# Masking the second attention's queries on ScalarE, padding two weights of layer 3 to 128 rows, and a new table of stages: a four-layer kernel on one core

## The reference, cut to what matters

```python
# layer 0: convolutions over tokens, cross-attention over channels (2 heads)
# layer 1: attention, 32 query heads of 8 numbers over 8 key heads, then norm; gamma, beta
# layer 2: attention of 16 heads of 16 numbers over 128 keys (context and own tokens), then the MLP
q = heads(x @ q_w + q_b);  k, v = split(concat(ctx, x) @ kv_w + kv_b)
s = q @ k.T / 16 ** 0.5 + mask              # per batch 16 heads x 64 queries x 128 keys
x = x + (softmax(s) @ v) @ out_w + out_b
x = x + gelu(rms(x) @ mlp_w1 + b1) @ mlp_w2 + b2
# layer 3: a recurrent block
xa = ln(x);  sx = shifted(xa) - xa
f = tanh((xa + sx * maa_x) @ maa_w1)        # 5 parts of 32 columns
xm_j = xa + sx * (maa_j + f_j @ maa_w2[j])  # the five mixings, a contraction over 32 each
w = exp(-exp(time_decay + tanh(xm_w @ td_w1) @ td_w2))      # decay, a contraction over 64
k, v, r = xm_k @ Wk.T, xm_v @ Wv.T, xm_r @ Wr.T;  g = silu(xm_g @ Wg.T)
for t in tokens:  a = outer(k_t, v_t);  out_t = r_t @ (u * a + s);  s = a + w_t * s
x1 = x + (groupnorm(out) * g) @ Wo.T
x = x1 + sigmoid(xr2 @ Wfr.T) * (relu(xk2 @ Wfk.T) ** 2 @ Wfv.T)   # xk2, xr2: shifted ln(x1)
```

## Time and profile before

| | |
|---|---|
| median of 3 runs | 1982.87 us (1982.61 to 1985.68) |
| the profiled execution | 1985.88 us |
| its span in the trace | 1984.2 us |
| mean granted clock of TensorE | 0.927 |
| busy, share of the span | PE 84%, PEld 52%, DVE 64%, ACT 47%, POOL 41% |
| chain that ended last | PE 58%, ACT 14%, DVE 11%, issue 8%, POOL 5%, DMA 2% |

### The profile page before, as it was taken

How to read it: one execution, slowest core, us unless ns; L and a number is a source line. 1 busy time by engine, 2 the same in 40 slices (tenths; PEclk the granted TensorE clock), 3 DMA queues, 4 the chain that set the end, 5 groups by cost and what they waited for, 6 DMA issues and landing times.

```text
span 1984.2 us, 36756 instructions
## 1 busy us (share of the span) xinstructions
PE 1676.4 (84%) x13615; PEld 1032.9 (52%) x13615; DVE 1276.6 (64%) x2183; ACT 932.2 (47%) x1831; POOL 805.1 (41%) x893
## 2 busy tenths in 40 slices
PE   5888898898988898888987989888988989888835
PEld 3565555564564555655555645646456554556203
DVE  3753469745796468845697457955689456883383
ACT  4444554544545544555445456454445454453202
POOL 4531247503573136701485034731367014750070
PEclk8998999999999999898999989998998989999757
DMA  6001014200332005210142103320052101410070
GB/s 177 2 1 34 1 23 50 38 24 1 42 37 38 18 1 64 26 27 18 22 47 29 37 1 37 41 39 18 1 60 29 27 18 19 48 23 12 0 86 11
DMA packets 73584, 60.92 MB, mean 31 GB/s; under 512 B 38960, under 2 KB 56512, under 8 KB 73408
## 3 DMA queue, kind: packets, MB, share of 16 engines
q1 hardware_dynamic: 55648, 47.99, 17.8%
q10 hardware_dynamic: 17216, 10.55, 2.1%
q0 software_dynamic: 544, 0.03, 0.0%
HBM read 20.28 MB, written 4.19 MB: 12 GB/s over the span
## 4 chain that ended last, share of the span: by engine, by line
PE 58%; ACT 14%; DVE 11%; issue 8%; POOL 5%; DMA 2%; ACTq 0%; DVEq 0%; POOLq 0%; SPq 0%
PE bank L622 24%; PE bank L761 7%; PE bank L1002 6%; PE bank L940 3%; PE bank L638 3%; PE bank L894 3%; ACT soft_ring L1141 3%; DVE late L1303 2%; DMA late<-late 2%; PE bank L701 2%; POOL soft_ring L1674 2%; PE bank L965 2%; DVE soft_ring L1450 2%; ACT soft_ring L1160 2%; ACT late L1032 2%
## 5 line engine op out<-in xcount | busy, mean ns | idle before, releaser
L1674 POOL TENSOR_TENSOR soft_ring<-soft_ring,seg_max 128x512 f32<-128x512 f32 x256 | 276.7, 1096 | 282.8 <-DVE seg_max L1456 282.1
L1160 ACT ACTIVATE soft_ring<-soft_ring 128x512 f32<-128x512 f32 x256 | 160.6, 627 | 234.9 <-POOL soft_ring L1674 223.0
L1632 POOL TENSOR_TENSOR late<-late 128x520 f32<-128x520 f32 x128 | 189.2, 1478 | 147.8 <-DMA late<-late 116.9
L1303 DVE TENSOR_TENSOR_SCAN late<-late 128x520 f32<-128x520 f32 x128 | 219.4, 1714 | 22.3 <-DVE xr L1481 6.7
L940 PE MATMUL bank<-ident,soft_ring 128*128 128x128 f32 x1024 | 170.3, 295 | 53.0 <-ACT soft_ring L1160 46.8
L940 PEld LDWEIGHTS bank<-ident,soft_ring 128*128 128x128 f32 x1024 | 116.3, 147 | 138.1 <-ACT soft_ring L1160 83.0
L1450 DVE SCALAR_TENSOR_TENSOR soft_ring<-bank,mask 128x512 f32<-128x512 f32 x256 | 164.0, 681 | 33.6 <-PE bank L761 25.9
L1456 DVE TENSOR_REDUCE seg_max<-soft_ring 128x8 f32<-128x512 f32 (+1 forms) x256 | 166.2, 674 | 5.8 <-DVE early L1514 2.1
L761 PE MATMUL bank<-early 64*128 64x512 f32 (+1 forms) x512 | 122.7, 566 | 55.4 <-ACTq L1144 51.2
L1682 POOL TENSOR_SCALAR soft_ring<-soft_ring,rden 128x256 f32<-128x256 f32 x64 | 62.2, 971 | 234.2 <-DVE rden L1423 234.2
L1032 ACT ACTIVATE late<-bank 128x512 f32<-128x512 f32 (+2 forms) x104 | 62.0, 597 | 202.1 <-PE bank L622 198.0
(11 more groups left out here) (250 smaller groups left out, 3402.5 us busy)
## 6 DMA issues: line engine op xcount, KB each, us to landing
late<-late SPq DMA_DIRECT2D x128, 260.0 KB, 4.4
c<-in_ctx ACTq DMA_DIRECT2D x8, 512.0 KB, 4.1
x<-in_x ACTq DMA_DIRECT2D x8, 512.0 KB, 5.2
out_x<-late SPq DMA_DIRECT2D x8, 512.0 KB, 2.9
mask<-in_mask_Bx1xSxS_ff ACTq DMA_DIRECT2D x16, 128.0 KB, 4.5
mask<-in_mask_BxS_ik SPq DMA_DIRECT2D x8, 256.0 KB, 3.4
w<-in_L_xattn_mlp_w SPq DMA_DIRECT2D x2, 1024.0 KB, 9.5
wkv<-in_L_xattn_kv_w SPq DMA_DIRECT2D x1, 512.0 KB, 4.4
```

Of the source, the lines that this page charges most:

```text
L1160: af(soft[:, u % SOFT, :], soft[:, u % SOFT, :], ACT.Exp).then_inc(sig("exp"), 1)
L1303: nc.vector.tensor_tensor_scan(sj[:, n % 2, :], wP[:, k, :, :].rearrange("p b t -> p (b t)"), aj[:, n % 2, :], 0.0, ALU.mult, ALU.add).the ...
L1632: tt(aj[:, n % 2, :], kP[:, k, :, :].rearrange("p b t -> p (b t)"), vj[:, n % 3, :], ALU.mult).then_inc(sig("kv_done"), 1)
L1674: tt(s, s, seg_max[:, u % SOFT, 0:segs].unsqueeze(2).broadcast_to([128, segs, 512 // segs]), ALU.subtract).then_inc(sig("sub"), 1)
```

## The change: masked queries from ScalarE, padded weights, new places

- **Queries.** `one_query` and `qring` are gone. ScalarE's drain of the queries writes them masked, twice (j = 0 and 1), into `qm`: heads of one parity each. Two heads share 32 partitions, so the scores now contract over 32 rows, and a bank of scores holds two head tiles times two batches in place of one batch with four. The mask is read for two batches at a time, and `pT2` is written accordingly. ScalarE takes 8 instructions a group in place of 4. The first half of the queries has a buffer of its own (`qm_first`).
- **Padding.** `maa2` and `td2` are filled up with zeros to 128 rows, and the products of the mixings and of the decay run over 128 rows. GpSimd zeroes 32 unused partitions of `xf` once per group (a wait for the previous group's last store ahead of it), and TensorE waits for that at a mixing.
- **Tables.** What table ScalarE has loaded is remembered from group to group.
- **Places.** Nearly every number of `PLACES` and `SCAN_PLACES` is another.

```diff
-        qring = sb("qring", [128, 2, KT, HPT // 2, L])
+        qm_first = sb("qm_first", [128, KT, NB // 2, 2, L])
...
-        q2T = cut(early, 7168, KT, NB, L)
+        qm = (qm_first, cut(early, 7168, KT, NB // 2, 2, L))
...
+                nc.gpsimd.memset(maa2[:, :, :], 0.0)
+                nc.gpsimd.memset(td2[:, :], 0.0)
...
-            "moments 2": (127, 128, 126, 121),
-            "turn 2": (132, 131, 130, 121),
-            "ffn k": (134, 133, 130, 122),
+            "moments 2": (127, 126, 125, 125),
+            "turn 2": (130, 129, 125, 128),
+            "ffn k": (133, 133, 129, 132),
...
+        loaded = [LOG_EXP]
...
                     def mix(f):
-                        rows = slice(32 * (f % 4), 32 * (f % 4) + 32)
                         for m in range(KT):
-                            product((stage, m), 512, [(maa2[rows, f // 4, 128 * m:128 * m + 128], xf[rows, f // 4, :])], "late")
+                            product((stage, m), 512, [(maa2[:, f, 128 * m:128 * m + 128], xf[:, f // 4, :])], "late")
...
-                            product((stage, m), 512, [(td2[64:64 + DD, 128 * m:128 * m + 128], xf[64:64 + DD, 1, :])], "late")
+                            product((stage, m), 512, [(td2[:, 128 * m:128 * m + 128], xf[:, 1, :])], "late")
...
-                    b = (u - UNITS) // 2
-                    pe.wait_ge(sig("k2_ready"), past("k2_ready") + 2 * (b // 4) + 2)
-                    pe.wait_ge(sig("qring_ready"), past("qring_ready") + b + 1)
+                    p, r = (u - UNITS) // 4, (u - UNITS) % 4
+                    pe.wait_ge(sig("k2_ready"), past("k2_ready") + 2 * (p // 2) + 2)
+                    pe.wait_ge(sig("q2_ready"), past("q2_ready") + p // 2 + 1)
                     side_by_side([("s", u), ("s", u + 1)], 4, lambda n, half: (
-                        qring[HALVES[half], b % 2, n // 2, 2 * (n % 2):2 * (n % 2) + 2, :], k2T[HALVES[half], n // 2, b, :]))
+                        qm[p // 2][32 * (r + half):32 * (r + half) + 32, n // 2, 2 * p % 4 + n % 2, :, :],
+                        k2T[32 * (r + half):32 * (r + half) + 32, n // 2, 2 * p + n % 2, :]))
...
                             for k in range(KT):
-                                ins = af(q2T[:, k, 4 * h:4 * h + 4, :], batches(t[:, 256 * k:256 * k + 256]), ACT.Identity, bias=v("q_b", k))
+                                for j in range(2):
+                                    ins = af(qm[h][:, k, :, j, :], batches(t[:, 256 * k:256 * k + 256]), ACT.Identity,
+                                             bias=q_bias[:, k, j:j + 1], scale=hmask2[:, j:j + 1])
...
-                def one_query(b):
-
-                    dve.wait_ge(sig("q2_ready"), past("q2_ready") + b // 4 + 1)
-                    if b >= 2:
-                        filled(("s", UNITS + 2 * b - 3))
-                    tt(qring[:, b % 2, :, :, :], q2T[:, :, b, :].unsqueeze(2).broadcast_to([128, KT, HPT // 2, L]),
-                       hmask4[:, :].unsqueeze(1).unsqueeze(3).broadcast_to([128, KT, HPT // 2, L]), ALU.mult).then_inc(sig("qring_ready"), 1)
...
+                        if before:
+                            pool.wait_ge(sig("stored"), past("stored"))
+                        link(nc.gpsimd.memset(xf[32:64, 1, :], 0.0))
+                        pool.sem_inc(sig("xf_zero"), 1)
```

More of the change, by code:

```diff
@@ L412, in _ @@
                 nc.vector.tensor_tensor(kvmask[:, :], block8[:, 0:8, 0], block8[:, 8:16, 0], ALU.add)
[L413 removed]
+                link(nc.vector.tensor_reduce(hmask2[:, :], hmask[:, :].rearrange("p (a j) -> p j a", j=2), X, ALU.add))
                 nc.vector.tensor_copy(ones2[:, 16:32], half[:, :, :].rearrange("p a b -> p (a b)"))
@@ L445, in build @@
             "moments": (0, 0, 0, 0),
[L446 to L466, removed]
-            "moments 2": (127, 128, 126, 121),
-            "normalize 2": (129, 131, 129, 121),
-            "turn 2": (132, 131, 130, 121),
-            "shift 2": (132, 131, 130, 121),
-            "ffn k": (134, 133, 130, 122),
-            "ffn r": (134, 133, 134, 128),
-            "ffn v": (134, 137, 134, 131),
+            "normalize": (3, 10, 1, 1),
+            "turn": (11, 11, 5, 1),
+            "shift": (14, 16, 12, 2),
+            "maa": (16, 16, 12, 7),
+            "mix 0": (17, 28, 18, 13),
+            "mix 1": (22, 28, 24, 13),
+            "td": (28, 30, 30, 19),
+            "k": (35, 30, 31, 19),
+            "mix 2": (35, 33, 35, 19),
+            "decay": (37, 36, 36, 19),
+            "v": (42, 40, 39, 23),
+            "mix 3": (42, 40, 42, 35),
+            "mix 4": (43, 40, 43, 36),
+            "r": (47, 44, 48, 39),
+            "g": (49, 48, 49, 41),
+            "r u k": (50, 49, 50, 41),
+            "bonus": (53, 51, 56, 57),
+            "center": (125, 122, 121, 119),
+            "variance": (125, 122, 121, 119),
+            "gate": (127, 122, 123, 119),
+            "project": (127, 126, 124, 121),
+            "moments 2": (127, 126, 125, 125),
+            "normalize 2": (127, 126, 125, 128),
+            "turn 2": (130, 129, 125, 128),
+            "shift 2": (132, 133, 128, 132),
+            "ffn k": (133, 133, 129, 132),
+            "ffn r": (133, 133, 132, 132),
+            "ffn v": (134, 133, 134, 132),
         }
         SCAN_PLACES = (
[4 rows of a table removed]
[4 rows of a table added]
         )
@@ L1519, in between @@
                             moments([xr[:, p, :] for p in (2 * h, 2 * h + 1)], stats[:, r, :], mv[:, r, :], "stats1_ready")
-                    if i == A2 - 1:
-                        for b in range(2):
-                            one_query(b)
                 def prepare(i):
@@ L1553, in prepare @@
                         dve.sem_inc(free, 1)
+                        for k in range(KT):
+                            ins = ts(q_bias[:, k, :], hmask2[:, :], v("q_b", k), None, ALU.mult)
+                        link(ins)
                         dve.sem_inc(sig("vec_ready"), 1)
@@ L1601, in vector_program @@
                     between(i)
-                    if A2 <= i < A2 + UNITS - 4 and (i - A2) % 2 == 1:
-                        one_query((i - A2) // 2 + 2)
                 if before is None:
```

34 lines of the change are left out of this document (22 added, 12 removed), and 8 rows, old and new, of the table SCAN_PLACES.

## The result

The changed kernel takes 1959.03 us (median of 4 runs, 1958.57 to 1961.88), the kernel before, measured again beside it, 1984.28. The ratio is 0.9863, 95% interval 0.9847 to 0.9879: 1.4% faster, 27 us. Forecast were 9. The direction and the range were right, the size was a third of what came.

The account below looks back on a forecast made before the run. TensorE was taken as the bound, other edits paying only through its waits; gains 3.8 less losses 3.0 gave 0.8 us a steady group, 5.6 in seven, plus group 0's 2.5: 8.1 off, forecast 1974 us, range 1950 to 1994.

Parts of the forecast that it names:

- the places' gain at the start of attention 2: TensorE's 4.67 us wait shrinks as scans and products run earlier: 0.9 us a group, bounds 0 and 4.67.
- the last block: Layer 3 of the last group alone: nothing competes there, so its time stays; no gain.
- Queries: Masking leaves VectorE: 0.65 us a group off the scores' wait in attention 2, plus 2.5 once in group 0.
- Scores over 32 rows: Attention scores: two tiles of 32 rows run side by side like those of 64, so nothing changes.
- rival 3: Score tiles of 32 rows don't run side by side: 0.6 us for each of 64 pairs, about 2012; chance 0.05.
- Padding: Mixings and decay over 128 rows: 10 fewer tile-mode changes at 0.17 us, 1.45 us a group taken; duration unchanged.
- The 0.8 for P0: GpSimd's product P0, placed ten subtractions later, no longer waits for its DMA: 0.8 us a group gained.
- P13 behind B: Recurrence behind attention 2: GpSimd's product P13 after bias row B delays scan 13; 1.6 us a group lost.
- MLP: TensorE waits 0.9 us before turn 2 and 0.9 before Wfk, less 0.4 gained: 1.4 us a group lost.
- Sum of the places: All new places: gains of 1.7 against losses of 3.0 us a group, so 9 us slower.
- Rival 1: VectorE bounds attention 2: its freed 8.3 us a group give 1917, or 1950 if half comes; chance 0.13.
- Rival 2: The new order waits at B ahead of P13 and the MLP's end: slower, 1996; chance 0.20.

Follow-up runs that it names:

- mix64: Changed kernel with the mixings over 64 rows (half of them zeros) in place of 128, decay still over 128: 1970 us, 0.9904 of the kernel before.
- scans_head: Kernel before with queries and padding changed, stages in old places, only the first 11 of 19 scan steps in new ones: 1956 us, 0.983 of before.
- p13_first: Changed kernel with one number changed, GpSimd's product P13 in front of the bias row B again: 0.9848 of the kernel before.
- mlp_old: Changed kernel with the stages from project on (project to ffn k, r, v) in their old places: 0.985 of the kernel before.
- all_but_queries: Changed kernel with VectorE's masking of the queries as before, padding and places as changed: 1976 us, 0.9953 of the kernel before.
- q_only: Kernel before with only the masked queries from ScalarE and the scores over 32 rows: 0.9964 of the kernel before, 7 us faster.
- pad_only: Kernel before with only the two weights padded to 128 rows: 0.9921 of the kernel before, 16 us faster.
- queries_pad: Kernel before with queries and padding changed, in the old places: 1955 us, 0.9845 of the kernel before.
- places_only: Kernel before with only the new numbers of the two tables of places: 1.0115 of the kernel before, 23 us slower.

## Why the prediction was wrong in size

Three terms of the sum were too small: padding (10 us), the places' gain at the start of attention 2 (0.9 us a group), and the last block (nothing). By stretches, the start of attention 2 and attention 2 itself shrank by 5.1 us a group where 0.9 + 0.65 were forecast, and the rest of a group grew by 2.4 where the terms gave 3.0 - 1.45 - 0.8 = 0.75. So the steady groups brought 1.9 us each more than forecast and the last block 5.6, and group 0 brought 0.9 less than its 2.5.

*Queries.* The mechanism held: VectorE was not the bound, TensorE waited at the start of attention 2 for GpSimd, and removing `one_query` alone moved that wait by 0.35 only. Forecast 0.65 x 7 + 2.5 = 7; alone it gave 7 (group 0: 3.1 shorter, forecast 2.5; 1.6 in the changed kernel). That is by luck, however: in the traced run, the slowest, TensorE spent 28.8 us of a steady group at 1.2 GHz, before 23.9, which at half speed is an estimated 2.4 us lost per group. Without the 32-row mixings the same part is worth 15 to 18 us (31 less 16, 27 less 9). That the 32 rows took the difference is likely by the last block, not shown for these stretches.

*Scores over 32 rows.* Right: 1.16 us for 16, rival 3 is out.

*Padding.* This is the first step that failed. "Duration goes by columns, not rows" is right for the product itself (3.20 and 3.21 us for six in the last block), and the price of the mode is of the right size as far as is known (1.45 a group forecast; 1.1 by `mix64`, not isolated). But I priced a product by its own duration and not by the clock of the products behind it. Forecast 10 us; 16 were measured alone and 32 on top of the others. Of these 32 most is attention 1, where with 32 rows the new places put 6.3 us a group at 1.2 GHz: it takes 45.8 us in place of 42.8, 21 us in seven groups. "Layer 3 of the last group alone has nothing that competes and stays" fell with it: 5.6 us.

*Places, gains.* The second step that failed. The wait of 4.67 fell by 3.3, where I took 0.9; I had both bounds and took the low end on the ground that the chain of scans and products has as many steps as before. It has: in both kernels the first subtraction of attention 2 stands on GpSimd behind P8. But the chain ends earlier: in group 5 that subtraction starts 66.5 us behind T0 before and 63.0 after. In the old order with the queries moved, GpSimd waits ahead of P8 for a scan:

```profile
1020.37 1.58 POOL L1636 TENSOR_TENSOR late<-late 128x520 f32<-128x520 f32 x1 [2.01 <-DVE late L1308]
1022.01 0.20 POOL L1638 COPY late<-s 128x8 f32<-128x8 f32 x1
1022.17 3.03 POOL L1678 TENSOR_TENSOR soft_ring<-soft_ring,seg_max 128x512 f32<-128x512 f32 x3
```

That scan stands on VectorE behind the first masks:

```profile
1015.94 1.29 DVE L1463 SCALAR_TENSOR_TENSOR soft_ring<-bank,mask 128x512 f32<-128x512 f32 x2 [2.37 <-PE bank L762]
...
1019.00 1.23 DVE L1308 TENSOR_TENSOR_SCAN late<-late 128x520 f32<-128x520 f32 x1
```

In the changed kernel the scan is ahead of the masks, and P8, without a wait, is ahead of the rows to add; the subtraction follows these:

```profile
1232.32 1.61 DVE L1310 TENSOR_TENSOR_SCAN late<-late 128x520 f32<-128x520 f32 x1 [0.31 <-DVE xr L1489]
...
1235.95 1.29 DVE L1465 SCALAR_TENSOR_TENSOR soft_ring<-bank,mask 128x512 f32<-128x512 f32 x2 [1.43 <-PE bank L766]
```

```profile
1234.77 1.28 POOL L1638 TENSOR_TENSOR late<-late 128x520 f32<-128x520 f32 x1
...
1239.25 3.03 POOL L1684 TENSOR_TENSOR soft_ring<-soft_ring,seg_max 128x512 f32<-128x512 f32 x3
```

By `scans_head` the places of the first 11 scan steps suffice for this: the start of attention 2 takes 22.1 us there. The stretch at 1.2 GHz behind the wait is gone in the changed kernel too, which no term had. The 0.8 for P0 is not to be seen in the sum: P0 starts at 1208.20 without a wait for its DMA, as forecast, but attention 1 idles 1.4 us more a group. TensorE's wait there for rows that VectorE normalises is 3.02 at 1218.02, where it was 0.81 at 1231.84.

*Places, losses.* The sizes were right. P13 behind B: forecast 1.6, by `p13_first` 1.5, though it is given back in attention 2, so that its worth in the whole is near nothing. MLP: forecast 0.9 + 0.9 less 0.4; the waits are 0.92 and 0.87, the stretch 1.4 longer than in `mlp_old`.

*Sum of the places.* Forecast 9 us lost. On the kernel before 23 are lost; with queries and padding about 4, less than the intervals tell.

*Rivals.* Rival 1 (VectorE the bound) gave a time nearer to the measured one at half its price, but its mechanism is not there. Its sign was badly chosen: the wait at the start of attention 2 did fall by more than 2 us, yet it falls to 1.69 in `all_but_queries` too, where VectorE masks as of old. Rival 2's waits came, and were outweighed. The prediction also drew on the Trainium skill ("GPSIMD Engine Reference", the table of the engine's figures), which has GpSimd contend for SBUF with VectorE's instructions of two SBUF inputs. For the masking this case does not bear it out: before, a subtraction wholly beside a masking took 1043 ns (8 of them), one with VectorE idle 1044 (16). After, the subtractions are no shorter (1135 ns on average, 1096 before), so nothing of the gain is from there. The copy behind P8 above does take 0.20 without a scan beside it, against 1.02 with one.

## What to carry to other kernels

Before summing durations, lay the granted clock beside the order of TensorE's products: a short product over few of the array's rows may cost nothing itself and be followed by full ones at half the clock (5.65 us for 3.60), while the same product padded with zeros took no longer. Look behind long waits as well: here 3.4 or 6.8 us at 1.2 GHz stood behind one of 4.67. Measure parts in pairs as well as alone when the clock is involved: here three parts of -7, -16 and +23 us made -27. And a wait removed by reordering is real only if the whole period shrinks; here corrections that took 1.4 and 1.5 us a group off their own stretch, alone and together, gave no measurable gain.

## What the runs showed of the hardware

- Products over 32 rows are followed by stretches at 1.2 GHz where those over 128 rows, of the same duration in the same order and with waits that differ by less than 0.5 us, are not. In the last block it is 0.80 against 1.00 over the same products, and 10.2 to 17.1 us at 1.2 GHz in four traces against none in eleven. In attention 1 of the new order it is 6.3 us a group against none.
- Products over 64 rows lie between (0.89 and 6.8 us in the last block; none behind T0 in attention 1).
- Where TensorE waited 4.3 to 4.7 us at the start of attention 2, its granted clock fell to 1.2 GHz between 3.0 us before the end of that wait and 0.4 us behind it, in all seven steady groups of each of four kernels (before, `q_only`, `pad_only`, `queries_pad`). In the changed kernel, with 1.4 us of wait there, it did in none. With 1.69 it did a little later in `places_only` and not in `all_but_queries`.
- A change of tile mode costs TensorE an estimated 0.1 to 0.2 us: 0.17 by rows 3, and 1.1 us for 8 changes more in a group by `mix64`, where the clock is not held equal.
- GpSimd's subtraction wholly beside VectorE's masking of queries took 1043 ns, with VectorE idle 1044; its copy of 8 columns beside a scan took 1.02 us in place of 0.20.
